# Two copies of V instead of three in the biased attention, and its V projection issued one unit later

## The reference, cut to what matters

```
x = x + 0.5 * channel_mix(layernorm(x))          # L0 ffn
x = x + biased_attention(layernorm(x))           # L0 attention: the stage that is changed
x = x + 0.5 * channel_mix(layernorm(x))
x = x + 0.5 * local_layers(layernorm(x))         # two layers of local attention and a gated ffn
x = x + gru(layernorm(x))                        # L1 attention: a gated scan over the tokens
x = x + 0.5 * local_layers(layernorm(x))
```

```
q, k, v = (h @ wq, h @ wk, h @ wv)  split into 16 heads of 64
scores  = q @ k.T + rel_emb[bucket(j - i)]       # 512 x 512 for each head and sequence
attn    = softmax(scores)                        # rows, float32
out     = (attn @ v) joined over heads @ wo
```

## Time and profile before

| | |
|---|---|
| median of 3 runs | 1273.77 us (1270.47 to 1277.51) |
| the profiled execution | 1270.47 us |
| its span, first to last instruction | 1268.6 us |
| PE busy | 1154.6 us, 91% of the span |
| DVE / ACT / POOL busy | 905.8 / 891.7 / 602.5 us |
| PE in the chain that ended last | 71% of the span |
| DMA, mean rate | 53 GB/s |

### The profile page before, as it was taken

How to read it: one execution, slowest core, us unless ns; L and a number is a source line. 1 busy time by engine, 2 the same in 40 slices (tenths; PEclk the granted TensorE clock), 3 DMA queues, 4 the chain that set the end, 5 groups by cost and what they waited for, 6 DMA issues and landing times.

```text
span 1268.6 us, 39845 instructions
## 1 busy us (share of the span) xinstructions
PE 1154.6 (91%) x15724; PEld 696.5 (55%) x15724; DVE 905.8 (71%) x2406; ACT 891.7 (70%) x2386; POOL 602.5 (47%) x396
## 2 busy tenths in 40 slices
PE   5899999999999977799999999898888899999995
PEld 1355555555555542476666666554555466666662
DVE  2498887887988845687777677757776577777762
ACT  5666666665766647587877787777878678877872
POOL 0265655665655521474655455333343345654540
PEclk8999999999999989899999999999999899999998
DMA  4622222222222214111211121011110111111101
GB/s 159 240 60 70 71 60 57 74 72 59 76 55 68 62 28 136 38 35 23 48 39 34 23 48 30 18 30 25 22 38 18 38 26 39 39 39 26 31 22 42
DMA packets 35657, 67.24 MB, mean 53 GB/s; under 512 B 6752, under 2 KB 8032, under 8 KB 35472
## 3 DMA queue, kind: packets, MB, share of 16 engines
q1 hardware_dynamic: 35472, 64.69, 19.3%
HBM read 15.32 MB, written 1.11 MB: 13 GB/s over the span
## 4 chain that ended last, share of the span: by engine, by line
PE 71%; ACT 10%; DVE 7%; issue 5%; DMA 3%; SPq 2%; POOL 1%; ACTq 0%; DVEq 0%; POOLq 0%
PE ps L481 11%; PE ps L462 8%; PE ps L1149 6%; PE ps L1079 5%; PE ps L1112 4%; PE ps L1020 4%; PE ps L1051 4%; PE ps L1030 4%; PE ps L1091 3%; PE ps L1021 3%; ACT arena L1260 3%; PE ps L1119 3%; PE ps L1155 3%; DMA arena<-arena 2%; PE ps L489 2%
## 5 line engine op out<-in xcount | busy, mean ns | idle before, releaser
L417 POOL TENSOR_TENSOR arena<-arena 128x1024 f32<-128x1024 f32 x128 | 241.0, 1893 | 173.1 <-DVE arena L595 173.1
L538 ACT ACTIVATE arena<-arena 128x512 f32<-128x512 f32 x256 | 182.5, 714 | 135.7 <-DVE arena L581 135.6
L978 POOL TENSOR_TENSOR arena<-arena 128x1024 f32<-128x1024 f32 x64 | 121.4, 1896 | 253.7 <-DVE arena L1394 253.7
L1260 ACT ACTIVATE arena<-arena 128x128 f32<-128x128 f32 x512 | 198.1, 390 | 44.9 <-DVE arena L1386 44.6
L581 DVE CUSTOM_DVE_ANT_0 arena<-ps,arena 128x512 f32<-128x512 f32 x256 | 164.3, 688 | 44.5 <-PE ps L462 41.9
L1386 DVE CUSTOM_DVE_ANT_0 arena<-ps,near,arena 128x128 f32<-128x128 f32 x512 | 144.1, 347 | 53.4 <-PE ps L1079 53.4
L481 PEld LDWEIGHTS ps<-arena 32*64 32x64 f32 x8192 | 122.8, 132 | 72.9 <-issue 43.8
L591 DVE STREAM_TRANSPOSE arena<-arena 128x1024 f32<-128x1024 f32 x128 | 156.8, 1233 | 2.5 <-POOL arena L417 2.0
L481 PE MATMUL ps<-arena 32*64 32x128 f32 x8192 | 140.5, 278 | 19.8 <-issue 14.7
L985 POOL TENSOR_TENSOR arena<-arena 128x1024 f32<-128x1024 f32 x64 | 150.9, 2358 | 0.7 <-PE ps L1051 0.7
L462 PE MATMUL ps<-arena 64*128 64x512 f32 x512 | 140.8, 632 | 2.8 <-issue 1.0
(11 more groups left out here) (127 smaller groups left out, 2070.7 us busy)
## 6 DMA issues: line engine op xcount, KB each, us to landing
arena<-arena SPq DMA_DIRECT2D x192, 128.0 KB, 2.4
arena<-arena SPq DMA_DIRECT2D x64, 192.0 KB, 2.6
arena<-rel_rows SPq DMA_DIRECT2D x16, 448.0 KB, 9.0
arena<-arena SPq DMA_DIRECT2D x64, 64.0 KB, 2.1
arena<-y SPq DMA_DIRECT2D x32, 128.0 KB, 2.3
arena<-arena SPq DMA_DIRECT2D x16, 127.8 KB, 2.4
arena<-in_wqkv SPq DMA_DIRECT2D x2, 768.0 KB, 6.5
x<-in_x SPq DMA_DIRECT2D x4, 256.0 KB, 4.7
```

What stands on the lines that cost most here:

```text
L417: nc.gpsimd.tensor_tensor(e, e, scale, ALU.mult).then_inc(self.normed, 1)
L538: nc.scalar.activation(self.e[:, r % 3, i, :], self.neg[:, i, :], ACT.Exp, bias=self.nmax[:, i:i + 1], scale=-1.0, accum_out=self.sums[:, ...
L1260: nc.scalar.activation(self.e[:, s, h, :], self.neg[:, h, :], ACT.Exp, bias=self.nmax[:, h:h + 1], scale=-1.0, accum_out=self.sums[:, s, h ...
```

## The change

`self.v` gets two buffers in place of three (u % 2). The projection of V and its copy out of PSUM are issued one unit later: in pass u PE and ACT do V of unit u+1 where they did V of unit u+2; q and k stay as they are. The waits are renumbered to that: `weigh(u)` asks for V of unit u+1 (not u+2) to have left PSUM, `copy_v(u)` asks for unit u-2 (not u-3) to have been weighed and spread. `self.pt` is carved right behind `self.e` instead of last. SP's waits are the same. (A blank line is gone too, so from there on line numbers are one lower.)

```
-        self.v = k.carve(3, self.GROUPS, NT, P)
+        self.v = k.carve(2, self.GROUPS, NT, P)
...
         self.e = k.carve(3, 4, T)
+        self.pt = k.carve(4, NT, T)
...
-        self.pt = k.carve(4, NT, T)
...
-            v = self.v[:, u % 3, :, :, :].rearrange("p j t c -> p j (t c)")
+            v = self.v[:, u % 2, :, :, :].rearrange("p j t c -> p j (t c)")
...
-            if u >= 3:
-                pe.wait_ge(self.ot_made, u - 2)
+            if u >= 2:
+                pe.wait_ge(self.ot_made, u - 1)
             for t in range(NT):
...
-                pe.wait_ge(self.v_read, min(u + 3, self.UNITS))
+                pe.wait_ge(self.v_read, min(u + 2, self.UNITS))
...
             if u + 2 < self.UNITS:
                 q_proj(u + 2)
                 k_proj(u + 2)
-                v_proj(u + 2)
             if scores:
+                v_proj(u + 1)
                 score(r + 1, 1)
...
-            if u >= 3:
-                act.wait_ge(self.weighed, u - 2)
-                act.wait_ge(self.v_spread, 96 * (u - 2))
-            nc.scalar.activation(self.v[:, u % 3, 0, :, :].rearrange("p a b -> p (a b)"), V, ACT.Copy).then_inc(self.v_read, 1)
+            if u >= 2:
+                act.wait_ge(self.weighed, u - 1)
+                act.wait_ge(self.v_spread, 96 * (u - 1))
+            nc.scalar.activation(self.v[:, u % 2, 0, :, :].rearrange("p a b -> p (a b)"), V, ACT.Copy).then_inc(self.v_read, 1)
...
             if u + 2 < self.UNITS:
                 copy_q(u + 2)
                 copy_k(u + 2)
-                copy_v(u + 2)
             if scores:
+                copy_v(u + 1)
                 exp(r + 1, 2)
```

More of the change, by code:

```diff
@@ L480, in weigh @@
                         cols = slice(h * DK, (h + 1) * DK)
-                        last = nc.tensor.matmul(ps[cols, T5_W + a, 0:P], self.v[rows, u % 3, (a - c) % self.GROUPS, c // self.GROUPS, cols],
+                        last = nc.tensor.matmul(ps[cols, T5_W + a, 0:P], self.v[rows, u % 2, (a - c) % self.GROUPS, c // self.GROUPS, cols],
                                                 self.pt[rows, u % 2 * 2 + h, :, keys],
```

## The result

The changed kernel is slower. Its median is 1285.23 us (1282.14 to 1287.64, 5 runs), beside 1273.77 us before; taken on the same chips in turn, with more runs (22 of the changed kernel, median 1282.19 us), the ratio is 1.0062, with a 95% interval of 1.0039 to 1.0087. That is a loss of 5 to 11 us; the two medians of fewer runs would give 1.0090. The forecast was 1270 us, the range ended at 1284. The profiled execution took 1282.15 us, its span is 1280.3 us, 11.7 us more than before.

A forecast was written before the change was run, and what follows sets the result against it. PE's list sets the stage's pace, with breaks where its next 16 KB piece is late; -2.2 (borders) + 1.4 (spread) - 0.1 (start) = -0.9 us on 1270.47 gave 1269.6, said as 1270 us, range 1263 to 1284.

The forecast's parts named there:

- The steady pass, the buffers, the arena: Attention stage and arena: same instructions and durations, V's waits see the same events, `pt` moves by two buffers; 0.
- The borders: PE's list in half A: borders between pieces fall 16 instructions later, nine breaks instead of ten; -2.2 us.
- Rival 1: PE's list: nothing depends on the borders, breaks stay as they are, transfers harmless; 1270.5 us, chance 0.13.
- The spread: SP's six transfers, now beside `weigh`: 0.15 us for each of nine breaks, +1.4 us; bounds 0 to +31 us.
- the clock: PE's granted clock: one drop more or less of about 1.5 us, either way, outside the sum.
- I am wrong if ordinary passes change their length: Sign against the forecast in the profile after: the pass without a break should still take 11.81 us.
- Rival 2: Half A and half B: the spread delays the pieces of PE's list; 1283 to 1299 us, chance 0.13.
- Rival 3: Half A: the breaks came from the spread and vanish with its move; 1248 us, chance 0.06.
- rival 4: Half A: V is late and it waits for the spread; 1 us per pass would give 1300 us, chance 0.02.
- Start and end: Stage's first scores start earlier, -0.1 us; at its end the extra V projection and copy are hidden, 0.

The follow-up runs named there:

- e2: Changed kernel with three buffers for V again, projection still one unit late: 1284.28 us, ratio 1.0089 to the kernel before.
- e11: Changed kernel, but SP issues the spread after the scores between the halves of `weigh`: 1270.86 us, ratio 0.9978 to the kernel before.
- e3: Changed kernel plus four matmuls with unused result at the stage's start, putting the borders back: 1286.19 us, ratio 1.0106 to the kernel before.
- e1: Kernel before with one SP wait edited, so the spread is issued 0.4 us before half A: 1285.25 us, ratio 1.0113 to the kernel before.
- e5: Changed kernel with spread transfers of 64 of 512 columns, same issues, result not the reference's: 1275.28 us, ratio 0.9996 to the kernel before.
- e6: Kernel before with spread transfers of 64 of 512 columns, issued after half B as ever, result not the reference's: 1274.60 us, ratio 0.9989.
- e4: Changed kernel, but SP issues a unit's spread only after half B of the unit before: 1290.42 us, ratio 1.0138 to the kernel before.
- e7: Kernel before with `weigh` in three parts (5, 5, 6 of 16 steps), scores between them: 1280.70 us, ratio 1.0033 to the kernel before.

## Why the prediction was wrong

**The steady pass, the buffers, the arena: 0.** Right. e2 shows that the third buffer doesn't matter, and e11, with two buffers and `pt` moved, has no loss. The usual pass without a break is 11.81 us in both.

**The borders: one break less, -2.2 us.** Right in the mechanism, wrong in the count. The list comes in pieces, and a shift of 16 instructions moved every break by 8 matmuls, there (after) and back (e3). The count looked at half A alone. A border 278 instructions into a pass is followed by one at 534, right behind half B, and PE can be late there too. The trace before has it in the seventh pass, where the scores behind half B took 2.12 us instead of 1.13, and the pass 12.75 instead of 11.81:

```profile
154.23 2.12 PE L462 MATMUL ps<-arena 64*128 64x512 f32 x4
```

So eleven passes lost more than 0.5 us before, not ten. After the change the two that were to fall out of the range, now at 278 and 282, still lost 2.4 and 0.6 us (the first has the break at 207.30 above), the one at 294 lost nothing, and again eleven passes lost more than 0.5 us. Nor does e11 show the -2.2: the 30 passes of its profiled execution took 378.0 us beside 376.5 before, with one stretch of half clock more, and why its median is 3.6 us lower (ratio 0.9978, interval up to 0.9998) is open. No run shows that the new places of the borders are worth anything. Rival 1 has fallen by the places of the breaks, and with it, for this stage, the "mostly hidden" of the Trainium skill (Runtime: NRT & Kernel Launch, section "Instruction fetch mechanics"): 14.7 us idle at L481 before.

**The spread: +1.4 us.** This is the step that failed, by its size. It was read correctly that the issues move to 0.4 us before half A, that V still lands in time, and that the transfers then run where pieces are fetched. I took 0.15 us for each of the breaks, nothing for the passes without, and nothing for the clock. Measured in the same two traces:

- The breaks in half A last 2.16 us on average (seven of them, 1.74 to 2.42) instead of 1.61 (eight, 1.31 to 1.96): 0.55 us each, not 0.15.
- Ordinary passes pay 0 to 0.4 us as well. By the prediction's own last sentence ("I am wrong if ordinary passes change their length") that was the sign.
- There was more half clock: 13.6 us of it instead of 3.4. The prediction had priced a stretch, but only as noise of either sign. It isn't a fixed part of the loss: e3's profiled execution is as long (span 1280.5 us) and has 6.8 us of half clock between 75 and 450 us.

Together with all else the 30 passes took 11.5 us more, where the sum had 1.4 for the spread and -2.2 for the borders. The number 0.15 was a choice near the lower end of 0 to 1.04. It was argued from one long issue of SP as the exception; the trace before had more of them: 11 of the 192 issues took over 0.9 us, and each overlapped a fetch; after it was 30. But the length of SP's issues is no price for PE either, since e11 has 27 such issues and no loss. What costs is a fetch that meets the spread in half A, where the next piece is awaited, and the trace before had none. Its rows left the term open between 0 and 31 us, and the range should have said so. Rival 2's 1283 us comes near the measured time, but in part by luck: it takes off a break that wasn't saved, and puts 0.5 us on every pass, where ordinary passes paid 0 to 0.4 us and those with a break more.

**Rival 2** (the spread delays the pieces, 1283 to 1299 us) was the right story, with a chance of 0.13. Its details were half right: half A pays, but half B hardly ever stops, and a part of the price is the clock. e1 (one wait on SP), e5 (bytes) and e11 (another time for the transfers) show it from three sides. What exactly holds a fetch up was not settled. Over all fetches the transfer is hardly longer (1.17 us beside the spread, 1.10 otherwise); the packet-by-packet turn that the Trainium skill states (DMA: Bandwidth & Descriptors, "Queues, rings and completion order") would allow a wait before it, but no run here measures it. Of the seven breaks in half A, four had a fetch that began late, 1.6 to 2.0 us into half A instead of 0.8 to 1.4; the other three had one that began in time but took 1.4 to 1.7 us instead of the 0.9 to 1.3 of before.

The records of fetches also show something that the prediction's story of the breaks lacks. The breaks give the borders, and from these one can count on to all others. Before, 59 of the 68 fetches began within 1.5 us of PE's passing a border. The eight in front of the breaks in half A began 2.1 to 7.3 us behind the last border, and all of them 0.8 to 1.4 us behind the start of half A. So a piece is not only used up fast there; its fetch also starts late. What it waits for is open; the waits of `weigh` stand in the list at that place, and no run moved them.

**Rival 3** fell with e6, **rival 4** with the waits after: no wait of L480 for a transfer. e4 shows how near it was: there were 6 us of reserve, and issuing some 6.5 us later (in e4 the spread starts 6.1 us into the pass, in the changed kernel 0.4 us before it) used all of them.

**Start and end.** The start gained 0.1 us as said. The end was put at 0 and cost 1.1 us: PE stood idle for 3.7 us by "issue" in the last two units and before for 1.5, and the last spread now runs into them.

## What to carry to other kernels

When a change moves when transfers are issued, ask what else they will run beside: an engine's own instruction list comes in by transfers too, and a stretch of many tiny matmuls (here 256 instructions in 2.1 us) can use it up faster than it comes. Look for idle time released by "issue" at places that shift by a constant number of instructions from pass to pass; such a stretch wants no bulk transfer beside it. And an interaction that the trace of before hardly shows isn't small because it is rare there: count how often it will happen after the change and give the bounds. Here these were 0 and 31 us, I put 1.4, and 11.5 were measured. When rows leave a term that open, the range has to be as wide, or an experiment has to come first: e1, one wait in the kernel before, would have told.

## What the runs showed of the hardware that was not expected

- A piece of PE's list is 16 KB, 256 instructions: the breaks in half A, before and after, lie whole multiples of 256 of PE's recorded instructions apart (its waits counted), and a pass has 580 of them. From the end of its transfer to the first instruction of it that runs behind a break are 1.2 to 1.5 us, in all breaks looked at.
- An issue of SP's that overlaps such a fetch can take longer: of the changed kernel's 192 issues 30 took 0.9 to 2.3 us instead of 0.6, and each of the 30 overlapped a fetch; 22 others overlapped one and kept their 0.6.

```profile
460.74 2.32 SPq L406 DMA_DIRECT2D arena<-arena  x1
```

- Going from 32x64 matmuls to 64x128 ones and back costs PE 0.46 us per pair of changes (e7), so finer interleaving isn't free.
- Four breaks of 2.03 to 2.23 us in the changed kernel were followed at once by 3.4 us of granted half clock, as at 163 us above; before, that happened once, behind a break of 1.60 us. The length of the break alone doesn't decide it: the changed kernel's two longest, 2.42 and 2.36 us, were followed by none, and e11 had it behind 1.69 and 1.75 us.
